# A graph network on one core: the first edge loop in another order, scores in three bf16 parts, edge transposes one group ahead

## The reference

```python
h = relu(layernorm(x)); hW = (h @ W.T).reshape(N, 4, 32)
att = einsum(hW[src], a_src) + einsum(hW[dst], a_dst)      # one score per edge and head
x = x + segment_sum(leaky_relu(att)[..., None] * hW[src], dst)
h = relu(layernorm(x))
e = concat([h[src], h[dst], edge_attr])
x = x + segment_sum(relu(e @ W_weight + b_weight) * sigmoid(e @ W_gate + b_gate), src)
```

## Time and profile before

| | |
|---|---|
| median of three runs | 5865.9 us |
| profiled execution | 5868.12 us |
| its span | 5866.5 us |
| mean granted TensorE clock, share of full speed | 0.912 |
| PE / PEld busy | 81% / 67% |
| DVE busy | 58% |
| ACT busy | 30% |
| POOL busy | 62% |

### The profile page before, as it was taken

The page is one execution under the profiler, slowest core; times in us unless marked ns, Lnnn a source line. Parts: engine busy times, 40 slices in busy tenths (PEclk is TensorE's granted clock), DMA queues, the critical chain, the costliest instruction groups (busy, mean ns, idle before and its releaser), DMA issues.

```text
span 5866.5 us, 125850 instructions
## 1 busy us (share of the span) xinstructions
PE 4757.8 (81%) x36031; PEld 3901.3 (67%) x36031; DVE 3391.2 (58%) x7758; ACT 1769.1 (30%) x3582; POOL 3661.0 (62%) x3930
## 2 busy tenths in 40 slices
PE   6488888988888888889888888888888857777773
PEld 2377777777777777658777777777777745555552
DVE  7777777777777777752222222222222269888885
ACT  0222222222222222333222322223222334444442
POOL 1277777777777777347777777777777733333332
PEclk8788888888888888899999999999999989999997
DMA  1333223222222222365555555555555478888887
GB/s 36 128 70 71 69 70 69 70 69 69 68 69 69 69 68 68 107 225 177 170 169 168 167 170 170 168 168 168 171 168 167 152 236 265 249 250 243 249 249 230
DMA packets 442315, 849.11 MB, mean 145 GB/s; under 512 B 121444, under 2 KB 262202, under 8 KB 442287
## 3 DMA queue, kind: packets, MB, share of 16 engines
q1 hardware_dynamic: 200623, 422.52, 24.3%
q0 software_dynamic: 179312, 392.12, 23.5%
q10 hardware_dynamic: 62352, 34.15, 1.9%
HBM read 542.52 MB, written 305.89 MB: 145 GB/s over the span
## 4 chain that ended last, share of the span: by engine, by line
PE 32%; DMA 26%; POOL 16%; issue 13%; ACT 5%; DVE 4%; POOLq 2%; ACTq 1%; DVEq 0%; SPq 0%
POOL parts L551 16%; DMA x<-xn 11%; DMA parts<-rows,sidx 8%; PE ps L704 7%; PE ps L693 7%; PE ps L731 5%; DMA late<-xn 3%; ACT earlier L924 3%; PE ps L691 3%; ACT rows L941 2%; DMA x1w<-x 2%; PE ps L669 2%; PE ps L683 1%; PE ps L707 1%; PE ps L715 1%
## 5 line engine op out<-in xcount | busy, mean ns | idle before, releaser
L551 POOL DMA_INDIRECT parts<-rows,sidx x1664 | 1636.9, 984 | 525.3 <-issue 444.3
L533 POOL DMA_INDIRECT gat<-table,sidx x1664 | 1584.2, 952 | 535.5 <-issue 510.1
L784 PE MATMUL ps<-w_edge,eat 128*128 128x256 f32 x3328 | 1003.7, 383 | 0.0
L786 PE MATMUL ps<-nodes_w,to_edge 128*128 128x256 f32 x3328 | 991.2, 379 | 0.0
L1321 DVE COPY rows<-srcf 128x8 f32 x208 | 45.2, 217 | 1513.4 <-DMA parts<-rows,sidx 1513.3
L941 ACT ACTIVATE rows<-ps 128x512 f32<-128x512 f32 x832 | 434.7, 602 | 1473.0 <-DMA parts<-rows,sidx 1393.8
L786 PEld LDWEIGHTS ps<-nodes_w,to_edge 128*128 128x128 f32 x3328 | 633.2, 190 | 86.3
L784 PEld LDWEIGHTS ps<-w_edge,eat 128*128 128x128 f32 x3328 | 617.1, 190 | 77.3
L1195 DVE TENSOR_SCALAR to_edge<-ps,iota_p 128x1024 f32<-128x1024 f32 x417 | 535.4, 1284 | 86.2 <-PE ps L669 73.7
L704 PE MATMUL ps<-msg,to_node 128*128 128x128 f32 x3328 | 577.1, 344 | 2.7 <-DVE msg L1244 2.7
L693 PE MATMUL ps<-hot 128*128 128x256 bf16 (+7 forms) x1664 | 571.8, 431 | 0.0
(11 more groups left out here) (201 smaller groups left out, 7259.3 us busy)
## 6 DMA issues: line engine op xcount, KB each, us to landing
rows<-parts SPq DMA_DIRECT2D x208, 1056.0 KB, 5.8
ea<-in_edge_attr SPq DMA_DIRECT2D x414, 256.0 KB
gat<-table,sidx POOLq DMA_INDIRECT x1664
nodes_w<-table_b SPq DMA_DIRECT2D x208, 128.0 KB
parts<-rows,sidx POOLq DMA_INDIRECT x1664
nodes_w<-table_a SPq DMA_DIRECT2D x416, 64.0 KB, 4.2
x1w<-x ACTq DMA_DIRECT2D x208, 64.0 KB
x<-x1o ACTq DMA_DIRECT2D x208, 64.0 KB
```

The costliest lines, as they stand in the source:

```text
L533: nc.gpsimd.indirect_dma_start(out=gat[:, s, j * TW:(j + 1) * TW], out_offset=None, in_=table0, in_offset=bass.IndirectOffsetOnAxis(ap=sid ...
L551: nc.gpsimd.indirect_dma_start(out=parts, out_offset=bass.IndirectOffsetOnAxis(ap=sidx[:, s, j:j + 1], axis=0), in_=rows[:, s, j, :], in_o ...
L784: pe.matmul(z, eat[:, j // 4, (j % 4) * P:(j % 4 + 1) * P], w_edge[:], start=True, stop=False)
L786: mmi = pe.matmul(z, to_edge[:, s % 2, j * P:(j + 1) * P], nodes_w[:, s, :], start=False, stop=True)
```

## The change

**First loop, order.** TensorE's step now is `turn_keys` and `sum_messages` of the group before, then `find_places` of the group two before, then scores, `spread_rel` and `match_keys`. On VectorE `pick` moves from the middle of the step to its end. The window of x1 is no longer added by a matmul: VectorE adds it (`add_sums`) while it takes the sums out of PSUM, last in its step.

**Scores.** A destination score is stored as three bf16 numbers that add up to the f32 one. In the first node stage ScalarE writes the leading part and an f32 copy (`sd_rest`), and VectorE splits the rest (`split_scores`, three instructions a tile, one tile late). In the loop `to_edge` is written as bf16, and each block takes three bf16 matmuls of four columns in place of one f32 matmul.

**One-hots.** `hot` has four buffers for two and is laid out with the 128 values of a block side by side (`hot_j`), where they stood 8 elements apart. The key turning becomes a PE transpose into bf16 PSUM, and ScalarE waits for all eight blocks. `hot_t` has two buffers.

**Scattering loop.** TensorE transposes the edge attributes of group q + 1 before the products of group q; `eat` has two buffers, laid over the space of `gat`. ScalarE evicts in the same order.

PSUM banks are dealt out anew: scores and places go to bank 4 beside the sums.

```diff
             def turn_keys(s, q):
                 pe.wait_ge(hot_up, q + 1)
                 for j in range(J):
-                    twice = hot[:, s % 2, :, :, j].rearrange("p d b -> p (d b)")
-                    pe.matmul(ps[:, 2 + j // 4, (j % 4) * P:(j % 4 + 1) * P], twice, ident_b[:],
-                              start=True, stop=True).then_inc(turned_ps, 1)
+                    twice = hot_j[:, s, j].rearrange("p r b -> p (r b)")
+                    pe.transpose(turned_b[:, j, :], twice, ident_b[:]).then_inc(turned_ps, 1)
...
             def sum_messages(s, q):
...
                 for j in range(J):
-                    pe.matmul(out_ps, to_node[:, s % 2, j * P:(j + 1) * P],
-                              msg[:, s % 2, j * F:(j + 1) * F], start=(j == 0), stop=False)
-                pe.wait_ge(x1_in, 16 * (q + 1))
-                pe.matmul(out_ps, ident[:], x1w[:], start=False, stop=True).then_inc(acc_up, 1)
+                    mmi = pe.matmul(out_ps, to_node[:, s % 2, j * P:(j + 1) * P],
+                                    msg[:, s % 2, j * F:(j + 1) * F], start=(j == 0), stop=(j == J - 1))
+                mmi.then_inc(acc_up, 1)
...
             def by_dst_step(s, q, turn, w, first):
                 if s > 0 or not first:
                     pe.wait_ge(digits_up, q)
-                    pe.wait_ge(picked_up, q + 1 if s == 1 and first else q)
-                    if s > 1 or not first:
-                        find_places((s - 2) % U, q - 2)
                     turn_keys((s - 1) % U, q - 1)
                     sum_messages((s - 1) % U, q - 1)
+                    if s > 1 or not first:
+                        pe.wait_ge(picked_up, q)
+                        find_places((s - 2) % U, q - 2)
                 pe.wait_ge(to_edge_up[0], q + 1)
                 pe.wait_ge(sdw_in[s], 16 * (turn + 1))
                 for j in range(J):
-                    mmi = pe.matmul(ps[:, 6, j * HEADS:(j + 1) * HEADS],
-                                    to_edge[:, 0, j * P:(j + 1) * P], sdw[:, s, :], start=True, stop=True)
+                    for k in range(3):
+                        mmi = pe.matmul(ps[:, 4, SCORES + j * HEADS:SCORES + (j + 1) * HEADS], to_edge_b[:, j * P:(j + 1) * P],
+                                        sdw[:, s, k * HEADS:(k + 1) * HEADS], start=(k == 0), stop=(k == 2))
                 mmi.then_inc(expanded, 1)
...
+            def turn_edges(s, q, turn):
+                pe.wait_ge(ea_in[s], 32 * (turn + 1))
+                for h in range(2):
+                    pe.wait_ge(ea_t, 2 * q + h + 1)
+                    for j in range(4 * h, 4 * h + 4):
+                        mmi = pe.transpose(ps[:, 2 + h, (j % 4) * P:(j % 4 + 1) * P],
+                                           ea[:, s, j * F:(j + 1) * F], ident[:])
+                    mmi.then_inc(ea_tp, 1)
+
+            def edge_products(s, q, f, turn):
+                pe.wait_ge(to_edge_up[1], f + 1)
+                spread_rel(1, f + 2)
+                pe.wait_ge(bw_in[s], 16 * (turn + 1))
+                pe.wait_ge(ea_t, 2 * q + 4)
...
...
+                turn_edges(0, w * G, w * GU)
...
+                        turn_edges((s + 1) % U, q + 1, turn if s < U - 1 else turn + 1)
+                        edge_products(s, q, q + w, turn)
...
+            def split_scores(t, s):
+                rest = sd_rest[0:PN, s]
+                dve.wait_ge(node_out, t + 2)
+                nc.vector.tensor_tensor(rest, rest, sd0[0:PN, s, :, 0, :], ALU.subtract).then_inc(scores_dve, 1)
+                dve.wait_ge(scores_dve, 2 * t + 1)
+                nc.vector.tensor_copy(sd0[0:PN, s, :, 1, :], rest).then_inc(scores_dve, 1)
+                dve.wait_ge(scores_dve, 2 * t + 2)
+                nc.vector.tensor_tensor(sd0[0:PN, s, :, 2, :], rest, sd0[0:PN, s, :, 1, :],
+                                        ALU.subtract).then_inc(scores_up, 1)
...
+            def add_sums(q):
+                dve.wait_ge(acc_up, q + 1)
+                dve.wait_ge(x1_in, 16 * (q + 1))
+                nc.vector.tensor_tensor(x1o[:], ps[:, 4, 0:F], x1w[:], ALU.add).then_inc(copied0, 1)
...
             def by_dst_step(s, q, g, turn, w, first):
...
                 if last:
                     dve.wait_ge(counts_ps, q)
-                    if s > 1 or not first:
-                        pick((s - 2) % U, q - 2, g - 2)
                     split_run((s - 1) % U, q - 1, w)
                 one_hot(s, g).then_inc(hot_up, 1)
                 dve.wait_ge(rel_up[0], f + 1)
                 dve.wait_ge(copied0, q + 1)
                 by_edge(s, iota_ps).then_inc(to_node0, 1)
+                if last:
+                    dve.wait_ge(expanded, U + q + 1)
+                if s > 1 or not first:
+                    dve.wait_ge(places_ps, q - 1)
+                    pick((s - 2) % U, q - 2, g - 2)
+                if last:
+                    add_sums(q - 1)
```

More of the change, by code:

```diff
@@ L759, in _ @@
             pe.wait_ge(b_second, 2 * T + 2)
+            def turn_edges(s, q, turn):
[11 more added lines that the diff above has]
+                pe.wait_ge(ea_t, 2 * q + 4)
+                for k in range(4):
+                    pe.wait_ge(part_up, 4 * q + k + 1)
+                    for j in range(2 * k, 2 * k + 2):
+                        z = ps[:, 4 + k, (j % 2) * 2 * F:(j % 2 + 1) * 2 * F]
+                        pe.matmul(z, eat[:, s % 2, j // 4, (j % 4) * P:(j % 4 + 1) * P], w_edge[:],
+                                  start=True, stop=False)
+                        mmi = pe.matmul(z, to_edge[:, s % 2, j * P:(j + 1) * P], nodes_w[:, s, :],
+                                        start=False, stop=True)
+                    mmi.then_inc(z1_up, 1)
             with pe.Fori(0, passes) as w:
                 spread_rel(1, w * G + w + 1)
-                with pe.Fori(0, GU) as i:
+                turn_edges(0, w * G, w * GU)
+                with pe.Fori(0, GU - 1) as i:
                     turn = pe.snap(w * GU + i)
@@ L929, in _, with evict_turned, evict_rows @@
             nodes(1)
+            def evict_turned(s, q):
+                for h in range(2):
+                    act.wait_ge(ea_tp, 2 * q + h + 1)
+                    nc.scalar.activation(eat[:, s % 2, h, :], ps[:, 2 + h, :], ACT.Copy).then_inc(ea_t, 1)
+            def evict_rows(s, q, turn):
+                act.wait_ge(placed[s], 16 * J * turn + 32)
+                for k in range(4):
+                    act.wait_ge(z1_up, 4 * U + 4 * q + k + 1)
+                    nc.scalar.activation(rows[:, s, 2 * k:2 * k + 2, 0:2 * F],
+                                         ps[:, 4 + k, :].rearrange("p (j f) -> p j f", j=2),
+                                         ACT.Copy).then_inc(part_up, 1)
             with act.Fori(0, passes) as w:
-                with act.Fori(0, GU) as i:
+                evict_turned(0, w * G)
+                with act.Fori(0, GU - 1) as i:
                     turn = act.snap(w * GU + i)
@@ L1158, in node_outs, with step @@
                                             ALU.add).then_inc(b_second, 1)
+            def split_scores(t, s):
[7 more added lines that the diff above has]
+                                        ALU.subtract).then_inc(scores_up, 1)
             def nodes(layer):
-                def step(i, s, last=False):
+                def step(i, s, last=False, first=False):
                     if not last:
                         normalise(layer, XU * i + s + 2, (i + 1) if s >= XU - 2 else i, (s + 2) % XU)
+                    if layer == 0 and not first:
+                        split_scores(XU * i + s - 1, (s - 1) % XU)
                     if layer == 1:
@@ L1168, in nodes @@
                 normalise(layer, 1, 0, 1)
-                with dve.Fori(0, T // XU - 1) as i:
+                for s in range(XU):
+                    step(0, s, first=s == 0)
+                with dve.Fori(0, T // XU - 2) as i:
                     for s in range(XU):
-                        step(i, s)
+                        step(i + 1, s)
                 for s in range(XU):
                     step(T // XU - 1, s, last=s == XU - 1)
+                if layer == 0:
+                    split_scores(T - 2, (T - 2) % XU)
+                    split_scores(T - 1, (T - 1) % XU)
                 if layer == 1:
```

144 lines of the change are left out of this document (68 added, 76 removed).

## The result

The changed kernel takes 5805.2 us (median of 7 runs, 5795.1 to 5825.8) against 5855.3 (5839.5 to 5871.1) for the kernel before on the same chip: ratio 0.9908, 95% interval 0.9885 to 0.9932. That is about 50 us faster. The forecast was 38 us faster, 5828 us in all, so the sign was right and the size too small.

What follows compares the result with a forecast made beforehand. TensorE was taken to bound the first loop, just above GpSimd's gathers, VectorE the node stage and GpSimd the scattering loop. -54.5 + 13.4 + 2.9 = -38.2 gave 5828 us against the median of 5865.9; range 5809 to 5864.

Steps and rivals of the forecast that it cites:

- What bounds the loop: First loop: TensorE sets the step at 10.33 us, GpSimd's gathers lie 0.3 us below and would bound it next.
- The signs named for this loop: First loop: gathers at 1.253 to 1.257 us, none awaiting `sidx`; `lin` awaiting gathers nearly always; TensorE never awaiting `earlier`.
- The first loop, -54.5: First loop including its drain: becomes bound by gathers at 1.255 us each, taking 2099.4 us in place of 2153.9.
- The reasons given for it: First loop, TensorE's step: cheaper scores save 1.1 us and the vanished wait for `earlier` 1.0, giving 8.2 us.
- The node stage, +13.4: First node stage: three added VectorE instructions cost 16.3 us, 3.8 of it hidden, plus 0.9 at the end; bounds 5 and 22.
- The scattering loop, +2.9: Start of the scattering loop: first scatter comes 2.9 us later, bounds 0 and 5; steady pace unchanged.
- The phase lock: First loop: `digits` hits a gather in every group, costing up to 0.24 us each, +50 in all, 5878 us; 8%.
- TensorE's clock: First loop: idle TensorE drops to 1.2 GHz, its step reaches about 11.3 us, +198, total 6080 us; 3%.
- What the Trainium skill says of transposes: First loop: a PE transpose does not count as activity for TensorE's clock, and `turn_keys` becomes one; no separate size.
- No gain: First loop: a new VectorE wait keeps the step at 10.3 us, leaving only the additions, +16, 5882 us; 7%.
- More than forecast: First node stage: its additions hide behind ScalarE and the loads, total 5815 us; 10%.

Runs made afterwards that it cites:

- the kernels with six gathers: Six gathers a group instead of eight: changed kernel 5415.5 us, on a slow chip 6825.8 and 6856.7; kernel before, on a slow chip, 6693.2.

## Why the prediction was right or wrong

**What bounds the loop: right.** TensorE set it, 0.3 us above the gathers; with the wait for `earlier` gone, gathers set it. The signs named for this loop came: no gather waits for `sidx`, `lin` waits in all 208 steps, no wait for `earlier` until the last group. The first gather stood at 300.1 and 297.6, not at 303 to 304.

**The first loop, -54.5: the term that was mis-sized.** The two profiles of each kernel give -58.9 (2153.9 to 2094.9) and -74.9 (2171.4 to 2096.5), -67 in the mean. The side after was 3 to 4.5 us off (forecast 2099.4): the pace is 1.2526, that of the gather-bound start, and I had taken a value toward the 1.257 of the earlier trace rows, where some gathers reach 1194 ns; after, none of 400 passes 957. The side before was the larger miss: I subtracted from one execution as if its length were fixed. The loop of before, in its two profiles (us, busy PE, PEld, DVE, ACT, POOL, PEclk, DMA, GB/s):

```profile
290.26:2444.11 2153.85, 1927.73 (x17462) 1640.25 (x17463) 1629.59 (x3114) 573.61 (x1040) 1584.18 (x1664) 0.84 0.29 68
...
290.04:2461.44 2171.40, 1942.21 (x17462) 1649.59 (x17463) 1628.28 (x3114) 574.81 (x1040) 1582.44 (x1664) 0.84 0.30 68
```

As many matmuls (17462 recorded in each) kept TensorE busy 14.5 us longer, of the 17.5 us between the loops, and VectorE and GpSimd were busy no longer. Steps of one execution differ too, and with them the granted clock (first profile, four steps, same columns):

```profile
970.90:981.80 10.90, 9.39 (x88) 7.65 (x86) 7.75 (x15) 2.85 (x5) 8.39 (x9) 0.75 0.30 68
981.80:993.20 11.40, 10.48 (x86) 9.16 (x85) 7.84 (x15) 2.74 (x5) 8.52 (x9) 0.79 0.32 76
1025.40:1035.70 10.30, 9.38 (x87) 8.06 (x86) 7.99 (x15) 2.74 (x5) 7.83 (x9) 0.83 0.33 78
1046.20:1056.00 9.80, 8.79 (x83) 7.50 (x82) 7.77 (x15) 2.74 (x5) 7.44 (x8) 0.91 0.30 69
```

Steps are longer where more of them runs at the lower of the clock's two levels, though not in proportion. That the clock also makes the 17.5 us between the two loops is likely and not shown: both means read 0.84, and the two profiles are from two chips. In the changed kernel TensorE has 3.5 us a step to spare, and its two loops differ by 1.6 us.

**The reasons given for it: half right.** I credited 1.1 us a step to cheap scores and 1.0 to the wait. TensorE's step came out at 6.5 us (10.02 less 3.52 of idle time), just under the forecast's 6.8 to 9.3, and VectorE's at 8.2 and not 8.6. The run with the order alone shows the loop at the gathers' pace with neither cheaper scores nor cheaper keys. The other way round, the old order with cheap matmuls also reached the gathers, so either half would do, but there the phase lock came in.

**The node stage, +13.4: right in size, by two errors that cancel.** It is 12.0 inside the stage. The three instructions take 0.50 us in most tiles (240.73 to 241.23) and not 0.65, and next to nothing of them is hidden: VectorE's wait for the root went from 11.9 to 11.1 us, where I took 3.8 off. In single profiles the first gather moved by anything from +7 to +19, since the work ahead of the stage ends between 197 and 208 us by itself.

**The scattering loop, +2.9: right.** 3.5 and 4.4 from loop end to first scatter in the two pairs, 3.0 of them by the run without it; pace unchanged.

**The sum, and the step that failed.** The first two profiled executions are 63.7 us apart: first gather +9.8, first loop -58.9, from its end to the first scatter +3.5, third loop -17.7. The second two, from different chips, are 65.4 apart: +7.5, -74.9, +4.4, -2.4. The medians differ by less, 50.1 and 54.1 us: the profiled executions of before lay 12.8 and 4.6 us above their own medians. The step that failed is the term of the first loop, -54.5 in the sum, which measured -58.9 and -74.9. Beside it the third loop, which the sum holds at nothing, was shorter by 17.7 and 2.4 us. How the 12 us that the forecast's -38.2 lacks against the medians divide between the two stays open; in the first pair the third loop is the larger part. The rest of the distance from 5828 to 5805.2 is the base: 5865.9 was the median of three runs, and that of seven is 5855.3. The lower end of 5809 had room for neither.

**The rivals.** The phase lock (8%, +50) did not come here and did come in the old order, at 22.6 us: not all steps were hit, and few at the full 0.24. That it stayed away here was close, and in part luck: `digits` starts 0.6 to 0.85 us into a gather, where the prediction had 0.5 and the stretch that lengthens gathers ends near 0.46. TensorE's clock stayed at a mean of 0.84 in the loop, and after alike, in spite of 3.5 us of idle time a step. What the Trainium skill says of transposes ("TensorE: Matmul & The Clock Gate", Part 4) changed nothing that shows in this mean. No gain (7%) is refuted by `lin`'s waits. More than forecast (10%, 5815) was nearest to the result, for another reason than the one given: the node stage hid less than supposed, not more.

## What to carry to other kernels

When one engine bounds a loop by a few per cent over another, find the wait inside its step before making its work cheaper: here the order, without cheaper matmuls, was worth the whole gain, and the 16-bit scores only cost 12 us elsewhere and, on the slower chips, went with a longer step. A saving against a loop that two engines nearly share should be taken from two or three profiles of before, as its length is not fixed (2153.9 and 2171.4 us here). And when a loop becomes bound by one engine's steady beat, the phase of other operations to it becomes nearly fixed too, so moving two small instructions can cost or save a stretched operation in most rounds.

## What was not expected of the hardware

The same program took 5852 to 5874 us in four series and 7322 to 7360 on three other chips, with TensorE's granted clock at 0.91 and 0.79, and a change that gains 0.9% on the first kind lost 1.2% on one of the second. Fewer gathers made those chips' steps shorter (12.5 against 15.5 us) though TensorE's instructions were the same; whether data transfers and the supply of instructions meet somewhere was not tried further and stays open. From gather 881 on, the first profile of before also had nine pauses of GpSimd, eight of 1.88 us and one of 1.76, 96 gathers apart, with no wait behind them. The kernel after, whose GpSimd never waits for `sidx`, has none; nor have the kernels with six gathers, whose GpSimd does wait, so waiting alone does not bring them.
